# Combining the outputs of more token tiles inside the expert stage, two tiles at a time, in a transformer block with 16 experts on one Trainium2 core

## The reference

```
h = layernorm(x) * (1 + ca) + sa
x = x + ga * attention(h)            # 16 heads, 4 sink keys and a window of 128
h = layernorm(x) * (1 + cb) + sb
scores = sigmoid(h @ gate_w.T)       # 16 experts
w, idx = top_k(scores, 2); w = w / (sum(w) + 1e-20) * 2.5
routed = sum over the 2 chosen experts of  w * ((silu(h @ w_gate) * (h @ w_up)) @ w_down)
shared = (silu(h @ ws_gate) * (h @ ws_up)) @ ws_down
out = x + gb * (routed + shared)
```

## Time and profile before

| | |
|---|---|
| median of 3 runs | 342.06 us (339.71 to 345.51) |
| profiled execution, own time | 338.69 us |
| its span | 336.8 us |
| mean granted clock of PE | 0.911 |
| busy PE / DVE / POOL / ACT | 277.9 / 232.6 / 202.8 / 164.7 us |
| mean traffic | 177 GB/s |

### The profile page before, as it was taken

One profiled execution on the slowest core, in us unless ns is written; L12 is line 12 of the kernel. 1 busy time (PEld: TensorE's weight loads), 2 busy tenths in 40 slices (PEclk: granted clock), 3 DMA queues, 4 the chain that ended last, 5 costly groups with the idle time before them and its releaser, 6 DMA issues.

```text
span 336.8 us, 5976 instructions
## 1 busy us (share of the span) xinstructions
PE 277.9 (83%) x1665; PEld 215.8 (64%) x1666; DVE 232.6 (69%) x900; ACT 164.7 (49%) x518; POOL 202.8 (60%) x254
## 2 busy tenths in 40 slices
PE   3897889997999889898896899999999999885000
PEld 3274457674857568574763689899999987674000
DVE  0477568798879966798769865645545687664990
ACT  3142472267435571257512456556666676554550
POOL 3604115756786586555745776566565688775981
PEclk9996997899989995899969999999999999999555
DMA  7939100115616346931217795555557789869793
GB/s 267 340 118 360 34 3 31 64 35 175 199 64 190 96 140 220 278 84 47 80 64 225 225 260 158 162 156 172 182 163 214 248 246 270 257 187 347 249 352 137
DMA packets 41436, 59.78 MB, mean 177 GB/s; under 512 B 5092, under 2 KB 29880, under 8 KB 41404
## 3 DMA queue, kind: packets, MB, share of 16 engines
q1 hardware_dynamic: 34312, 39.91, 40.8%
q0 software_dynamic: 6528, 17.90, 14.9%
q10 hardware_dynamic: 564, 1.59, 1.4%
HBM read 33.57 MB, written 25.80 MB: 176 GB/s over the span
## 4 chain that ended last, share of the span: by engine, by line
PE 43%; DVE 31%; DMA 10%; issue 5%; ACT 4%; POOL 4%; SPq 1%; POOLq 0%; DVEq 0%; ACTq 0%
PE bank L1246 12%; PE bank L910 6%; PE bank L1256 6%; PE bank L1103 6%; DMA p_win<-slots 4%; PE bank L1070 4%; DVE bank L1769 3%; DVE h_sb L1389 3%; PE bank L1047 2%; DVE st L1363 2%; DMA ys<-pt_win,row_i 2%; DMA ht<-in_L_attn_x_dram 2%; PE bank L1085 2%; DVE xs L1411 2%; PE bank L953 2%
## 5 line engine op out<-in xcount | busy, mean ns | idle before, releaser
L605 POOL DMA_INDIRECT slots<-h_sb,slot_i x64 | 63.2, 987 | 31.5 <-DVE slot_i L1460 16.3
L1246 PE MATMUL bank<-ht,w_now 128*128 128x128 f32 x576 | 76.2, 275 | 0.6 <-DVE xs L1411 0.6
L1246 PEld LDWEIGHTS bank<-ht,w_now 128*128 128x128 f32 x576 | 70.1, 192 | 0.9 <-DVE xs L1411 0.8
L660 POOL DMA_INDIRECT ys<-pt_win,row_i x40 | 38.8, 971 | 22.1 <-ACT pt_win L688 16.6
L688 ACT ACTIVATE ht<-bank 128x256 f32<-128x256 f32 x104 | 39.6, 381 | 18.5 <-PE bank L910 17.5
L1758 DVE TENSOR_TENSOR act_t<-bank,sg 128x128 f32<-128x128 f32 x72 | 20.9, 290 | 37.8 <-ACT sg L857 37.3
L1103 PE MATMUL bank<-w_route,ht 128*128 128x272 f32 x128 | 41.6, 453 | 4.8 <-ACT ht L688 2.4
L1256 PE MATMUL bank<-w_dn,act_t 128*128 x144 | 43.4, 384 | 1.2 <-DVE act_t L1758 1.2
L660 POOL DMA_INDIRECT ys<-y_more,row_i x32 | 30.8, 964 | 16.8 <-ACT y_more L688 14.6
L910 PE MATMUL bank<-ident,p_win 128*128 128x128 f32 x198 | 35.7, 275 | 4.2 <-DMA p_win<-slots 2.4
L1643 DVE COPY w_now<-w_gu 128x512 f32 x75 | 34.8, 465 | 4.7 <-issue 4.6
(11 more groups left out here) (262 smaller groups left out, 524.7 us busy)
## 6 DMA issues: line engine op xcount, KB each, us to landing
p_win<-slots SPq DMA_DIRECT2D x67, 129.0 KB, 2.3
slots<-pads SPq DMA_DIRECT2D x28, 129.0 KB
xs<-in_L_attn_x_dram SPq DMA_DIRECT2D x3, 1024.0 KB
wmod_sb<-ys SPq DMA_DIRECT2D x12, 256.0 KB, 5.0
w_gu<-ys SPq DMA_DIRECT2D x10, 256.0 KB, 2.8
mod_bc<-mod_rows_out SPq DMA_DIRECT2D x4, 512.0 KB, 5.5
w_dn<-in_L_ffn_w_down_dram SPq DMA_DIRECT2D x1, 2048.0 KB, 10.8
h_sb<-ys SPq DMA_DIRECT2D x8, 256.0 KB, 4.0
```

The lines of the kernel that those rows point to most:

```text
L605: pool.indirect_dma_start(out=slots, out_offset=bass.IndirectOffsetOnAxis(ap=slot_i[:, k, j:j + 1], axis=0), in_=h_sb[:, j, :], in_offset= ...
L660: pool.indirect_dma_start(out=ys, out_offset=bass.IndirectOffsetOnAxis(ap=row_i[:, col:col + 1], axis=0), in_=y_sb[y], in_offset=None).the ...
L1246: last = mm(bank[2 + k % 2][:, half * P:(half + 1) * P], w_now[:, k, c, half * M:(half + 1) * M], ht[:, k, c, :], start=(c == 0), stop=(c ...
```

## The change

`weigh_at` takes every second expert tile from 46 to 52 as before, and then every one from 54 to 67: 18 token tiles (0 to 17) are combined inside the expert stage. For these, `gated`, `add_out` and `save` work on a pair of token tiles: one DVE instruction of 2 x 256 columns behind the second `both` of a pair, one POOL addition, one transfer. The semaphores of gate and addition count pairs there. `add_out` follows one expert tile after the second weighing, not two. On DVE `both` moves ahead of the weight copy, and `gated` behind the copy of the same tile. The weighing of the first tile of a pair waits until the pair before it is gated. KEEP is as before, so that SP stores a pair at every second expert tile from 56 to 66.

```
--- before.py
+++ after.py
@@ -279,8 +279,13 @@
             return started(h) if h >= FULL_BY else min(started(h) + EARLY, started(FULL_BY))
 
         def weigh_at(t):
-            d, odd = divmod(t - half_loaded(0) - LAG - 2, 2)
-            return d if d >= 0 and not odd and d < TILES else None
+            first, every = half_loaded(0) + LAG + 2, half_loaded(1) + LAG + 2
+            if t >= every:
+                return GROUP + t - every if t < SURE else None
+            return (t - first) // 2 if t >= first and (t - first) % 2 == 0 else None
+
+        assert all(weigh_at(t) is None or half_loaded(weigh_at(t) // GROUP) + LAG + 2 <= t for t in range(SURE))
+
 
         KEEP = half_loaded(0) + 2 * LAG + UNROLL
 
@@ -288,6 +293,15 @@
             return bank[4] if d < HEAD else bank[d % 2]
 
         HEAD = sum(weigh_at(t) is not None for t in range(SURE))
+        assert HEAD % PAIR == 0
+
+        def whole_pair(d):
+
+            return d < HEAD
+
+        def added(d):
+
+            return d // PAIR + 1 if whole_pair(d) else HEAD // PAIR + d - HEAD + 1
 
         names = """
         ld_cond ld_wmod ld_small ld_wqk ld_wv ld_ws ld_exp pad_dmas
@@ -334,6 +348,10 @@
 
         def got(d, n):
             return got_pair[d // PAIR][:, d % PAIR, n, :]
+
+        def got_first(d):
+
+            return got_pair[d // PAIR][:, :, 0, :] if whole_pair(d) else got(d, 0)
 
         def xcols(t):
             return xs[:, ds(t * D, D)]
@@ -463,12 +481,12 @@
             def load_rows(d):
                 p, i = divmod(d, PAIR)
                 if RING <= p < AHEAD:
-                    sp.wait_ge(S["out_ready"], (p - RING + 1) * PAIR)
+                    sp.wait_ge(S["out_ready"], added((p - RING) * PAIR + PAIR - 1))
                 sp.dma_start(got_pair[p][:, i], ys[d * TOPK * P:(d + 1) * TOPK * P, :]
                              .rearrange("(p n) d -> p n d", n=TOPK)).then_inc(got_sem(p)[0], 16)
 
             def save(t, n):
-                sp.wait_ge(S["out_ready"], t + n)
+                sp.wait_ge(S["out_ready"], added(t + n - 1))
                 b, j = divmod(t, TPB)
                 sp.dma_start(out[b, j * P:(j + n) * P, :].rearrange("(t p) d -> p t d", p=P),
                              xs[:, t * D:(t + n) * D].rearrange("p (t d) -> p t d", d=D)).then_inc(S["saved"], 16)
@@ -499,8 +517,8 @@
                     load_rows(loaded)
                     loaded += 1
                 if t >= KEEP and (t - KEEP) % 2 == 0:
-                    save(kept, 1)
-                    kept += 1
+                    save(kept, PAIR)
+                    kept += PAIR
                 if t == SURE - UNROLL:
                     last_owned, fours = tile_count(sp)
 
@@ -514,19 +532,18 @@
                 if d % GROUP == 0:
                     half_done(d // GROUP)
                 load_rows(d)
-            for t in range(kept, loaded // GROUP * GROUP):
-                save(t, 1)
-                kept += 1
+            for t in range(kept, loaded // GROUP * GROUP, PAIR):
+                save(t, PAIR)
             for k in range(UNROLL):
                 wait_apart(sp, y_out[k], (fours if k < UNROLL - 1 else fours + 1) * 16)
                 wait_apart(sp, xt_in[k], sp.snap(fours + OWN_FOURS) * 16)
             for d in range(AHEAD * PAIR, TILES):
                 load_rows(d)
-            for t in range(kept, TILES - GROUP, PAIR):
+            for t in range(loaded // GROUP * GROUP, TILES - GROUP, PAIR):
                 save(t, PAIR)
             for t in range(TILES - GROUP, TILES):
                 save(t, 1)
-            sp.wait_ge(S["saved"], 16 * (kept + (TILES - GROUP - kept) // PAIR + GROUP))
+            sp.wait_ge(S["saved"], 16 * ((TILES - GROUP) // PAIR + GROUP))
 
         @block.gpsimd
         def _(pool):
@@ -661,13 +678,18 @@
                                         in_=y_sb[y], in_offset=None).then_inc(done, 16)
 
             def add_out(d):
-                pool.wait_ge(S["gated_ready"], d + 1)
-                pool.tensor_tensor(xcols(d), xcols(d), got(d, 0), ALU.add).then_inc(S["out_ready"], 1)
+                if whole_pair(d) and d % PAIR == 0:
+                    return
+                pool.wait_ge(S["gated_ready"], added(d))
+                x = xcols(d)
+                if whole_pair(d):
+                    x = xs[:, ds((d - 1) * D, PAIR * D)].rearrange("p (t d) -> p t d", t=PAIR)
+                pool.tensor_tensor(x, x, got_first(d), ALU.add).then_inc(S["out_ready"], 1)
 
             for t in range(SURE):
                 pool.wait_ge(ex_y_sb[t % UNROLL], t // UNROLL + 1)
                 put(row_col(t), t % (2 * UNROLL), y_out_sem(t))
-                d = weigh_at(t - 2)
+                d = weigh_at(t - 1)
                 if d is not None:
                     add_out(d)
                 if t == SURE - UNROLL:
@@ -680,7 +702,7 @@
                     wait_apart(pool, ex_y_sb[k], n)
                     put(row_col(SURE + k), k, y_out[k])
 
-            for d in range(sum(weigh_at(t - 2) is not None for t in range(SURE)), TILES):
+            for d in range(sum(weigh_at(t - 1) is not None for t in range(SURE)), TILES):
                 add_out(d)
 
         @block.scalar
@@ -858,7 +880,9 @@
 
             def weigh(d):
                 act.wait_ge(*got_sem(d // PAIR))
-                if d > 0:
+                if whole_pair(d) and d % PAIR == 0 and d > 0:
+                    act.wait_ge(S["gated_ready"], added(d - 1))
+                elif d > 0:
                     act.wait_ge(S["both_ready"], d if d < HEAD else d - 1)
                 act.activation(first_bank(d)[:, 0:D], got(d, 0), ACT.Copy, scale=w_tok[:, d:d + 1])\
                     .then_inc(S["part_ready"], 1)
@@ -1770,9 +1794,14 @@
                                        first_bank(d)[:, 0:D], ALU.mult, ALU.add).then_inc(S["both_ready"], 1)
 
             def gated(d):
+                if whole_pair(d) and d % PAIR == 0:
+                    return
                 dve.wait_ge(S["both_ready"], d + 1)
-                v.tensor_tensor(got(d, 0), bank[5][:, d % 2 * D:(d % 2 + 1) * D], mbc(d // TPB, GB), ALU.mult)\
-                    .then_inc(S["gated_ready"], 1)
+                sums, gate = bank[5][:, d % 2 * D:(d % 2 + 1) * D], mbc(d // TPB, GB)
+                if whole_pair(d):
+                    sums = bank[5][:].rearrange("p (t d) -> p t d", t=PAIR)
+                    gate = gate.unsqueeze(1).to_broadcast([P, PAIR, D])
+                v.tensor_tensor(got_first(d), sums, gate, ALU.mult).then_inc(S["gated_ready"], 1)
 
             def loop_rows(u, k, n):
                 wait_apart(dve, y_out[k], (owned if k < UNROLL - 1 else owned + 1) * 16)
@@ -1791,11 +1820,11 @@
                     dve.wait_ge(S["tables"], 2)
                 if k == 1:
                     e = table(DVEE, t + 3, UNROLL, (NE - 1) * 2 * M)
+                if weigh_at(t) is not None:
+                    both(weigh_at(t))
                 ex_weights((k + 3) % UNROLL, e[(k + 3) % UNROLL])
                 if weigh_at(t) is not None:
-                    both(weigh_at(t))
-                if weigh_at(t - 1) is not None:
-                    gated(weigh_at(t - 1))
+                    gated(weigh_at(t))
                 if t < 2:
                     expert_table(2 + t)
                 if t == TABLE_AT or t == TABLE_AT + 1:
```

## The result

The changed kernel takes 350.5 us (median of 4 runs, 349.07 to 351.92), the kernel before 340.88 (4 runs): the ratio is 1.0278, with a 95% interval of 1.0234 to 1.0321. A second series, in which the kernel before took 346.76 us, gave 1.0331 (1.0272 to 1.0391). The forecast was 345.3 us, +1.0%, in a range of 339.5 to 351. So the direction was right and the size was not; the measured time lies at the range's upper end.

A forecast was written before the change was run, and what follows sets the result against it. It took the expert stage as paced by PE, with little room on POOL, DMA and SP's queue, and the tail by DVE. Terms +6.0, +0.5 and -3.25 summed to +3.25 us: forecast 345.3 us, +1.0%, range 339.5 to 351.

The forecast's parts named there:

- The store in SP's queue: Expert stage: SP's pair store waits for POOL's addition and holds the tile loads queued behind it; +6.0 us (+4 to +9).
- DVE, ACT and the pair's gate and addition: Expert stage until tile 60: longer gate and addition, DVE's moved copy and ACT's new wait; together +0.5 us (0 to 1.5).
- The sum: Whole span: +6.0 for the store, +0.5 for gate and addition, -3.25 for the tail, giving +3.25 us.
- Seven tiles in the stage at no cost: Expert stage: added row loads and stores fit DMA's room, ACT's seven more weighings its idle time; charged nothing.
- The tail: After the last expert tile: fewer token tiles left, counted from the last scatter in three terms; together -3.25 us.
- term a: Start of the tail: ACT's eviction of tile 71 no longer waits for an earlier scatter to land; -2.0 us.
- term b: Tail, from the last store's start to the first late load: 3.2 us in place of 3.93; -0.7 us.
- term c: Tail, from the first late load to tile 22's use: about 3.4 us in place of 3.95; -0.55 us.
- DVE becomes the bound: Rival, expert stage: a pair of tiles takes DVE 4.6 us in place of 3.86, +5.2, total 344; chance 0.10.
- PE's clock falls: Rival, expert stage: PE's stalls drop its clock to half, up to 3.1 us per fall, 348 to 351.5; chance 0.26.
- No hold: Rival, expert stage: SP's store does not hold the load back, leaving 339.3 us; chance 0.14.
- The signs that were named: Profile after: store waits about 4 us at tiles 60 and 64, PE idle about 3 before 61 and 65, clock at 1.00.

The follow-up runs named there:

- e15: Changed kernel with the weight copy ahead of the weighted sum and the pair addition cut to 4 of 256 columns, stores still early: 1.0135 of the kernel before.
- e11: Changed kernel with stores ten expert tiles late, copy ahead of the weighted sum, and pair addition cut to 4 of 256 columns: 0.9989 of the kernel before.
- e12: Changed kernel with stores ten expert tiles late and the pair addition cut, copy still behind the weighted sum: 1.0087 of the kernel before.
- e1: Changed kernel with one edit, SP stores a pair ten expert tiles after its second weighing: 1.0267 of the kernel before.
- e14: Changed kernel with only the stores ten expert tiles later, run again beside the unedited changed kernel on one chip: 1.0342 of the kernel before.
- e13: Changed kernel without any edit, run again on one chip: 1.0331 of the kernel before.
- e7: Kernel before with the new schedule alone, tile by tile without pairs, single stores ten tiles after weighing: 0.9974 of the kernel before.
- e2: Changed kernel with one edit, DVE's weight copy ahead of the weighted sum again, stores early: 1.0188 of the kernel before.
- e3: Changed kernel with stores ten expert tiles late and the copy ahead of the weighted sum, addition whole: 1.0110 of the kernel before.
- e6: Changed kernel with only POOL's pair addition cut to 4 of 256 columns: 1.0187 of the kernel before.
- e9: Changed kernel with late stores, copy ahead of the weighted sum, and the pair addition split in two halves behind two scatters: 1.0042 of the kernel before.
- e16: Changed kernel with late stores, copy first, pair addition split behind two scatters, and row numbers from one tensor: 1.0080 of the kernel before.
- e4: Changed kernel with late stores and only ten token tiles in the stage, at every second expert tile from 46 to 64: 1.0137 of the kernel before.
- e10: Kernel before with the new schedule alone, unpaired, and row numbers by an operation that reads one tensor: 0.9965 of the kernel before.
- e5: Changed kernel with late stores, copy ahead of the weighted sum, and row numbers by an operation that reads one tensor: 1.0110 of the kernel before.

## Why the prediction was wrong in size

- **The store in SP's queue, +6.0.** The mechanism exists, at the places that were given: in e15 against e11 tile 61 came 3.3 us later and tile 65 5.8, where +3.5 and +6.0 had been predicted. That the size agrees is in part luck: the addition is cut there, and the first fall of the clock, up to 1.7 us, lies between the two tiles and was not in the term. In the changed kernel this term is worth nothing that the runs can tell: taking it away left 1.0342 against 1.0331. Another hold lies over the same time.
- **DVE, ACT and the pair's gate and addition, +0.5 until tile 60 (0 to 1.5): the step that failed.** The gate of 512 columns was right (0.68 us, 0.7 predicted), the addition too (1.28, taken as 1.45). Wrong was the sentence that a copy which meets the addition "waits up to 0.7 longer, which lies inside the bounds just given and is not added". It took 2.04 us, 1.1 longer than the 0.96 of the earlier trace rows and 1.6 longer than by itself, and it did so in every pair, because DVE's new order puts it into the scatter ahead of the addition. Until the transposes of tile 60 the stage had lost 3.2 us, and the term was charged no further, since the stalls would leave DVE free; DVE was what stalled. With the late store this alone costs 1.0267 and 1.0342 against 0.9989 in e11, some 10 to 12 us. Most of it is the long addition: with the addition cut and the order kept, e12 is at 1.0087.
- **The reading behind that step.** The earlier trace rows had a copy of 0.96 beside a scatter and an addition. I read it as a copy that had met the store, and as the ceiling. It was one that got in between the two: it ended inside the addition. The copy at 278.07, which I took for one that met nothing, ran its whole 0.42 us inside another scatter, with no addition behind it (POOL's timeline of the kernel before):

```profile
277.93 0.99 POOL L660 DMA_INDIRECT ys<-y_more,row_i  x1 [0.16 <-issue]
```

  So the rows did not agree with a lock that the scatter holds for its whole length; what a copy meets is the addition, and the row for one of 512 columns was missing.
- **The sum.** I added terms as if each had its own place on the path. Here two holds run side by side, and they don't add: with copy and addition mended, the store costs 1.5% (e15 against e11); with the store mended, copy and addition still cost 2.8 to 3.5% (e1 and e14 against e11); all together cost 2.9 to 3.4% (the change and e13 against e11).
- **Seven tiles in the stage at no cost.** Missed: e7's stage is 2.5 us longer without pairs, beside a tail 3.1 shorter.
- **The tail, -3.25.** Right in the sum, -2.98, and in the mechanism; that the sum is so close is luck, since term a was 0.6 too large and term b 0.7 too small. From the product of tile 71 to the last scatter 3.03 us in place of 4.40 (-1.4, term a: -2.0), from there to the first late load 2.56 in place of 3.93 (-1.4, term b: -0.7), from there to its use 3.38 in place of 3.95 (-0.6, term c: -0.55). A second gap of DVE behind it, before the third late tile, gives 0.3 back.
- **The rivals.** "DVE becomes the bound" was given 0.10 and 4.6 us for a pair; it is the one that came nearest, at 5.0 to 5.3, because the copy takes 2.04 where the rival's upper end had 0.96. Its sign was not as named: PE's waits are put down to loads far more than to DVE (11.9 against 3.1 us), since it is the loads that wait for DVE's row numbers. "PE's clock falls" happened beside it: once in the profile after and once in that of e13, for up to 1.6 us, half of the price given, and behind two idle times of about 1 us each, where this rival had counted on PE standing for over 3. It was also seen in e1, e2, e12, e14 and e15; in e3 to e6, e9, e11 and e16 the clock stayed at 1.00 from 268 to 318 us. "No hold" is what e11 and e7 show: 0.9989 and 0.9974, where 339.3 us had been worked out, 0.8% under the time before.
- **The signs that were named.** PE's stalls end on the tile's load, as said (11.9 us in 13 waits), and the store waits are there (12.0 us in five). Both would have been taken for proof. Against it spoke the sizes at tiles 61 and 65 (1.16 and 0.36 us in place of about 3), the copy's 2.04 us, for which no sign had been named, and the clock, which was to stay at 1.00 between tiles 60 and 71.

## What to carry to other kernels

When two engines contend, price the operation that stands by the whole of the longest instruction that it can now meet, not by the meeting that an old trace happens to show, and look which operation a new order moves in front of that instruction. A wait that ends last in the trace is not the cause until its removal has been run: here the late load had two reasons at once, SP's store and the row numbers behind DVE's copy, and taking one away only changed the name of the releaser. Making one long instruction out of two short ones is no saving if another engine is shut out for its length. Here two of 256 columns let DVE in between, and one of 512 did not. POOL's addition one tile later, so that it meets another part of DVE's work, was not tried.

## What the runs showed of the hardware

- A DVE copy that began 0.52 us into a scatter on POOL with an addition of 512 columns 0.02 us behind it ended 0.30 us after the addition. Over all traces 35 copies began in such a scatter (in the change, e1, e4, e13 and e14), and all 35 did so, at 1.76 to 2.22 us.
- With an addition of 256 columns behind the scatter, 18 of 19 copies (in the kernel before, e7 to e10 and e16) ended inside the addition, at 0.42 to 1.05 us, as that of the earlier trace rows; the other, in e10, ended 0.29 us after it, at 1.23. With the addition cut to 2 x 4 columns (e6, e12) all 13 took 0.66 or 0.67. Whether the length decides, or that the 512 columns are two runs of 256 in one instruction, was not tried; the cut addition has two runs as well.
- With no addition right behind the scatter, copies that began in it took 0.41 to 0.66 us (439 in all traces).
- The two-input row-number operation was held in the same way (1.84 us for 0.21, e3); written with one input it took 265 and 266 ns in the mean in e5 and e16, and in e5 copies were held in its place.
- An addition of 512 columns on POOL took 1.28 us, one of 256 in the tail 0.72, and in the stage 0.74 to 0.82 in the mean (e7).
- In every stretch with a fall of the clock that I measured over six us (314 to 320 in the change, 296 to 302 in e13, 316 to 322 in e14, 302 to 308 in e12) the mean granted clock was 0.72, so a fall cost at most 1.7 us.
- One tile load took 5.6 us from its issue to PE's use of it in e12, with PE waiting, where 3.1 to landing is the median before; why is open.
